# State-space loop: GpSimd multiplies two states by two C rows in one operation of 2048 columns

## What is computed

```python
def step(h, inp):
    u_t, dt_t, B_t, C_t = inp
    h = jnp.exp(dt_t[:, :, None] * A) * h + (dt_t * u_t)[:, :, None] * B_t[:, None, :]
    y = jnp.einsum('bds,bs->bd', h, C_t)
    return (h, y)
...
y = ys.transpose(1, 0, 2) + u * Dp
y = y * jax.nn.silu(z)
return y @ W_out.T
...
x = x + _L0_conv_ref(_gn(x), ...)
x = x + _L1_conv_ref(_gn(x), ...)
```

## Time and profile before

| | |
|---|---|
| median of 3 runs | 5644.61 us (5643.97 to 5648.42) |
| the profiled execution | 5637.48 us, span 5635.7 us |
| the 64 chunks | about 100 to 3440 us of the span |
| busy over the span | PE 89%, DVE 80%, POOL 80%, ACT 61% |
| TensorE's clock in the loop | granted in full (1.00), 2.4 GHz |

### The profile page before, as it was taken

How to read it: one execution, slowest core, us unless ns; L and a number is a source line. 1 busy time by engine, 2 the same in 40 slices (tenths; PEclk the granted TensorE clock), 3 DMA queues, 4 the chain that set the end, 5 groups by cost and what they waited for, 6 DMA issues and landing times. The chain is left out here.

```text
span 5635.7 us, 68281 instructions
## 1 busy us (share of the span) xinstructions
PE 5006.5 (89%) x22742; PEld 2621.1 (47%) x22742; DVE 4530.2 (80%) x6402; ACT 3450.4 (61%) x4188; POOL 4494.9 (80%) x2067
## 2 busy tenths in 40 slices
PE   6999999999999999999999997982779999899898
PEld 3444444444444444444444444530446666566565
DVE  8999999999999999999999997005767677677665
ACT  5666676676676676666566562000667777677676
POOL 6999999999999999999999995001557777677676
PEclk9999999999999999999999999795889999999999
DMA  5656666566566555565566562592789999999999
GB/s 206 211 211 212 210 211 213 209 211 215 208 211 214 208 212 214 208 212 213 209 212 214 209 212 97 216 407 50 165 156 191 195 194 192 193 193 190 189 192 184
DMA packets 1416309, 1137.13 MB, mean 202 GB/s; under 512 B 1212666, under 2 KB 1222546, under 8 KB 1408532
## 3 DMA queue, kind: packets, MB, share of 16 engines
q1 hardware_dynamic: 1411480, 1131.52, 72.2%
q10 hardware_dynamic: 4478, 1.25, 0.2%
HBM read 814.23 MB, written 21.09 MB: 148 GB/s over the span
## 5 line engine op out<-in xcount | busy, mean ns | idle before, releaser
L822 POOL TENSOR_TENSOR mamba_state<-mamba_state,mamba_c_row 128x1024 f32<-128x1024 f32 x1024 | 2404.9, 2366 | 107.3 <-DVE mamba_state L795 96.8
L693 PE MATMUL mamba_y_ps<-mamba_state,ident 128*128 128x512 f32 x4096 | 1954.4, 602 | 146.9 <-POOL mamba_state L822 145.6
L795 DVE TENSOR_TENSOR_SCAN mamba_state<-mamba_decay,mamba_b_ps 128x1024 f32<-128x1024 f32 x704 | 1609.9, 2287 | 96.3 <-DVE mamba_b_ps L781 1.9
L1957 POOL TENSOR_TENSOR l3s_el<-l3s_s_sb,l3s_eh 128x1024 f16<-128x1024 f32 x512 | 1083.3, 2135 | 473.3 <-ACT l3s_s_sb L1942 454.3
L693 PEld LDWEIGHTS mamba_y_ps<-mamba_state,ident 128*128 128x128 f32 x4096 | 744.2, 189 | 995.6 <-issue 659.2
L1965 DVE TENSOR_SCALAR_CACHE_REDUCE l3s_s_sb<-l3s_s_ps 128x512 f32<-128x512 f32 x1024 | 705.3, 690 | 453.2 <-PE l3s_s_ps L1898 447.8
L1912 PE MATMUL l3s_o_ps<-l3s_vt,l3s_et 128*128 128x257 f16 x4096 | 806.0, 275 | 132.0 <-DMA l3s_et<-l3s_el 90.9
L781 DVE TENSOR_TENSOR mamba_b_ps<-mamba_dtu,mamba_b_ps 128x1024 f32<-128x1024 f32 x704 | 849.4, 1207 | 0.6 <-PE mamba_b_ps L681 0.6
L1941 ACT ACTIVATE l3s_eh<-l3s_s_sb,l3s_shift 128x1024 f16<-128x1024 f32 x512 | 583.5, 1140 | 429.3 <-DVE l3s_shift L1976 405.7
L795 DVE TENSOR_TENSOR_SCAN mamba_state<-mamba_b_ps,mamba_b_row 128x1024 f32<-128x1024 f32 x320 | 729.1, 2278 | 103.4 <-POOL mamba_b_row L816 103.3
L771 ACT ACTIVATE mamba_decay<-mamba_dt,mamba_A 128x1016 f32<-128x1016 f32 x704 | 782.9, 1133 | 12.5 <-DVE mamba_state L795 9.4
(11 more groups left out here) (325 smaller groups left out, 5153.7 us busy)
## 6 DMA issues: line engine op xcount, KB each, us to landing
mamba_c_row<-mamba_c_rows SPq DMA_DIRECT2D x1024, 512.0 KB, 3.8
mamba_b_row<-mamba_c_rows SPq DMA_DIRECT2D x320, 512.0 KB, 4.8
l_ring_a<-in_L_conv_W SPq DMA_DIRECT2D x28, 1024.0 KB, 11.0
l2b_ring_b<-in_L_conv_W SPq DMA_DIRECT2D x26, 1024.0 KB, 11.1
l_ring_a<-in_L_conv_W SPq DMA_DIRECT2D x14, 704.0 KB, 12.7
l2b_ring_b<-in_L_conv_W SPq DMA_DIRECT2D x13, 704.0 KB, 12.7
l_ring_a<-in_L_conv_W SPq DMA_DIRECT2D x14, 640.0 KB, 12.1
l2b_ring_b<-in_L_conv_W SPq DMA_DIRECT2D x13, 640.0 KB, 12.1
```

The costliest lines, as they stand in the source:

```text
L693: last = nc.tensor.matmul(y_ps[:, half(h)], C["ident"][:, :], state[:, s % STATES, half(h)], start=False, stop=(s == S - 1))
L795: nc.vector.tensor_tensor_scan(state[:, s % STATES, :], by, add, 0.0, ALU.mult, ALU.add).then_inc(s_scan, 1)
L822: nc.gpsimd.tensor_tensor(state[:, s % STATES, :], state[:, s % STATES, :], c_row[:, s % C_ROWS, :], ALU.mult).then_inc(s_hc, 1)
L1957: nc.gpsimd.tensor_tensor(el[:, part, off:off + EXPW], s_sb[:, par, j * EXPW:(j + 1) * EXPW], eh[:, part, off:off + EXPW], ALU.subtract).t ...
```

## The change

- GpSimd's product takes two units at once: at each even unit it multiplies the states of the two units before it, which lie in neighbouring buffers, by two C rows in neighbouring buffers (2048 columns). `pool_product` does nothing for odd units. C rows are loaded as before, one transfer each, but wait and signal in pairs.
- `LAG` is 4 (was 3), `STATES` 6 (was 4), `DECAYS` 3 (was 4), `GATE_AT` 3 (was 2).
- GpSimd makes the drives of units 3, 5, 7, 9, 11 (was 2, 4, 6, 8, 10), three units ahead (was two), and their B rows are loaded five units ahead (was two), those of units 3 and 5 both at unit 0.

```diff
-LAG = 3
-PAIRS, DECAYS, STATES, C_ROWS = 2, 4, 4, 4
+LAG = 4
+PAIRS, DECAYS, STATES, C_ROWS = 2, 3, 6, 4
+DUO = 2
-GATE_AT, OUT_AT, ADD_AT = 2, 14, 15
+GATE_AT, OUT_AT, ADD_AT = 3, 14, 15
-POOL_UNITS = (2, 4, 6, 8, 10)
+POOL_UNITS = (3, 5, 7, 9, 11)
-B_ROWS, DRIVE_AHEAD, B_LOAD_AHEAD = 5, 2, 2
+B_ROWS, DRIVE_AHEAD, B_LOAD_AHEAD = 5, 3, 5
...
+        def decay_free(c, s):
+            c_of, k = divmod(by_dve(c, s) - 1 - DECAYS, len(DVE_UNITS))
+            return c_of * S + DVE_UNITS[k] + 1
...
-            wait(sp, s_hc, unit + 1 - C_ROWS)
-            sp.dma_start(c_row[:, s % C_ROWS, :], c_dram[par, s].partition_broadcast(P)).then_inc(s_crow[s % C_ROWS], 16)
+            if s % DUO == 0:
+                wait(sp, s_hc, (unit - C_ROWS) // DUO + 1)
+            sp.dma_start(c_row[:, unit % C_ROWS, :],
+                         c_dram[par, s].partition_broadcast(P)).then_inc(s_crow[unit % C_ROWS // DUO], 16)
...
-            wait(pe, s_hc, unit + 1)
+            if s % DUO == 0:
+                wait(pe, s_hc, unit // DUO + 1)
...
-                wait(act, s_scan, unit + 1 - DECAYS)
-                to = decay[:, s % DECAYS, :]
+                wait(act, s_scan, decay_free(c, s))
+                to = decay[:, decay_slot(c, s), :]
...
-            wait(pool, s_scan, unit + 1)
-            wait(pool, s_crow[s % C_ROWS], 16 * (c * S // C_ROWS + s // C_ROWS + 1))
-            nc.gpsimd.tensor_tensor(state[:, s % STATES, :], state[:, s % STATES, :], c_row[:, s % C_ROWS, :],
+            if s % DUO:
+                return
+            own, row = unit % STATES, unit % C_ROWS
+            wait(pool, s_scan, unit + DUO)
+            wait(pool, s_crow[row // DUO], 16 * DUO * (unit // C_ROWS + 1))
+            nc.gpsimd.tensor_tensor(state[:, own:own + DUO, :], state[:, own:own + DUO, :], c_row[:, row:row + DUO, :],
                                     ALU.mult).then_inc(s_hc, 1)
...
-            if s + B_LOAD_AHEAD in POOL_UNITS:
-                load_b(sp, c, par, s + B_LOAD_AHEAD)
+            for k in POOL_UNITS:
+                if s == max(0, k - B_LOAD_AHEAD):
+                    load_b(sp, c, par, k)
...
-            late = behind(c, par, s, 1)
+            late = behind(c, par, s, DUO)
```

More of the change, by code:

```diff
@@ L577, in mamba_layers @@
         s_bdrive = sem(f"{tag}_pool_drive_ready")
-        s_crow = [sem(f"{tag}_c_row_loaded_{i}") for i in range(C_ROWS)]
+        s_crow = [sem(f"{tag}_c_rows_loaded_{i}") for i in range(C_ROWS // DUO)]
         s_hc = sem(f"{tag}_hc_ready")
@@ L690, in pe_sum @@
                     nc.tensor.matmul(y_ps[:, half(h)], weights(c)["diag_Dp"][:, :], u[:, par, half(h)], start=True, stop=False)
-            wait(pe, s_hc, unit + 1)
+            if s % DUO == 0:
+                wait(pe, s_hc, unit // DUO + 1)
             for h in range(2):
-                last = nc.tensor.matmul(y_ps[:, half(h)], C["ident"][:, :], state[:, s % STATES, half(h)], start=False,
+                last = nc.tensor.matmul(y_ps[:, half(h)], C["ident"][:, :], state[:, unit % STATES, half(h)], start=False,
                                         stop=(s == S - 1))
@@ L793, in dve_scan @@
                 wait(dve, s_drive, by_dve(c, s))
-                by, add = decay[:, s % DECAYS, :], b_ps[s % PAIRS][:, :]
-            nc.vector.tensor_tensor_scan(state[:, s % STATES, :], by, add, 0.0, ALU.mult, ALU.add).then_inc(s_scan, 1)
+                by, add = decay[:, decay_slot(c, s), :], b_ps[s % PAIRS][:, :]
+            nc.vector.tensor_tensor_scan(state[:, unit % STATES, :], by, add, 0.0, ALU.mult, ALU.add).then_inc(s_scan, 1)
         def dve_gate(dve, c, par):
@@ L951, in _ @@
                 run(pool, pool_unit)
-                pool_product(pool, LAST, LAST % 2, S - 1)
+                pool_product(pool, LAST, LAST % 2, S - DUO)
 GRID = 4
```

6 lines of the change are left out of this document (4 added, 2 removed).

## The result

The changed kernel takes 5675.48 us (median of 5 runs, 5671.87 to 5679.78), beside 5643.97 us for the kernel before (5 runs, 5640.04 to 5648.42): a ratio of 1.0056, 95% interval 1.0042 to 1.0071. It is slower by 31.5 us. The forecast was 5667 us, slower by 22, within a range of 5612 to 5700.

A forecast was written before the change was run, and what follows sets the result against it. It took TensorE, VectorE and GpSimd as nearly full, bound by a VectorE-GpSimd loop of 52.82 us a chunk. Loop +12, norm chunks +6 and the end +4 make +22 us: 5667 us, range 5612 to 5700.

The forecast's parts named there:

- the term of the loop: Chunk period from gate to gate over 63 periods: 53.01 us against 52.82, +12 us in all.
- The pair's price: GpSimd's 2048-column product, start to start: 4.47 us taken, upper bound 4.63, lower bound 3.55.
- The bound of 3.55: Lower bound in us for GpSimd's pair product, from the only 2048-column row (3595 ns); not taken.
- rival 1: GpSimd's pair is cheap: at the 3.55 bound a chunk takes 51.7 us, the kernel 5584 us; chance 0.15.
- The old loop: GpSimd's products delay its drives for VectorE's scans; opening it would leave VectorE's 51.07 us floor, 110 us less.
- The new chain: Gate to gate through GpSimd's pairs up to (8,9), then TensorE's queue to sum 15: 28.4 + 14.0 + 10.6 = 53.0 us.
- VectorE's side waits: VectorE waits for late B rows 8, 12, 13, 15; with these it alone would reach the gate at 52.3 us.
- rival 3: Nothing decides: pair at 4.42 us or slack in TensorE's chain, within 11 us of before, some 5650 us; chance 0.24.
- Norm chunks: TensorE's norm products behind the out product come onto the path, in 14 and 7 chunks: +6 us.
- The end: After the last scan a whole pair and two sums follow instead of one product and one sum: +4 us.
- Rival 2: TensorE is not late at the gate; B rows 13 and 15 set 52.3 us a chunk, 5622 us; chance 0.08.
- Rival 4: Four loads together are late, GpSimd starts pair (0,1) late: 1 us a chunk gives 5730 us; chance 0.08.

The follow-up runs named there:

- run 2: The changed kernel with one product a unit instead of pairs, everything else of the change kept: 5581.99 us, ratio 0.9893 to the kernel before.
- Run 1: The changed kernel with two idle TensorE matmuls put ahead of the sum of unit 6: 5648.42 us, ratio 1.0011 to the kernel before.
- run 11: The changed kernel with single products, TensorE also waiting before sum 6 for VectorE's drive of unit 10: 5743.89 us, ratio 1.0180 to before.
- run 9: Changed kernel, single products; bc product ahead of sum 1, dt product and sum 3 behind B row 8, GpSimd's first product after VectorE's norm operations: 5569.44 us.
- run 8: The changed kernel, pairs kept, with sums five units behind instead of four and the gate at 4: 5751.83 us, ratio 1.0190 to before.
- run 4: The changed kernel with the z product of the preparation moved ahead of sum 6 in TensorE's queue: 5736.01 us, ratio 1.0169 to before.
- run 5: The changed kernel with the z product ahead of sum 6 and the out product ahead of sum 8: 5683.16 us, ratio 1.0071 to before.
- run 10: The changed kernel with single products, TensorE's sum of an even unit still waiting for the next unit's product: 5582.01 us, ratio 0.9894 to before.

## Why the prediction was right, and where it was not

It forecast the sign, the mechanism and the place, and the time within 8.5 us. That the time came so near is in part luck: one large term was missing, and the term of the loop was too large.

- **The pair's price.** p = 4.47 forecast; from start to start the rows give 4.48 to 4.50, 4540 ns by the group. The bound of 3.55, and with it rival 1, is out. The figure of the Trainium skill (GPSIMD Engine Reference, section on performance versus the Vector engine), 4497 ns for this size, is 43 ns below the mean here.
- **The old loop opens.** Right: VectorE no longer waits for GpSimd's drives, and run 2 shows that the new places without the pair are worth 1 us a chunk.
- **The new chain, step by step** (clean chunk, gate at 2792.06). Pair (2,3) after 3.50 (3.48 forecast). TensorE sees pair (8,9) at 28.49 (28.4). B row 1 starts 13.71 later (14.0). Sum 15 ends 10.52 after that (10.54). The gate comes at 52.76 (53.0). VectorE's side waits were 0.43 at drive 8, 0.32 at 12 and 0.17 at 13 (0.6 and 0.1 to 0.3 each forecast). GpSimd idles 2.11 before pair (14,15) (2 forecast). B row 15 was in time. The chain is 0.25 shorter than the sum of pitches, the largest piece of it in the turn (0.36 us from start to start, 0.50 forecast), so the loop's +12 us is -3 (63 x -0.05). That is the term that was mis-sized: a difference of 15 us, the distance between rival 3 and the forecast.
- **Norm chunks.** +6 forecast. Run 1, whose loop is clean, has 63 periods from first scan to first scan with a mean of 52.95 over 52.77, 11.5 us; before has 52.87 over 52.82, 3.3. So +8.
- **The end.** +4 forecast, +3.9 measured: from the start of the last scan to the last gate are 10.66 us instead of 6.78. The intervals from gate to gate hide it (the last is 50.13 in run 1 and 50.29 before), because the gate of the chunk before has moved by one unit. VectorE's last scan and last gate, before and then changed:

```profile
3435.02 2.29 DVE L795 TENSOR_TENSOR_SCAN mamba_state<-mamba_decay,mamba_b_ps 128x1024 f32<-128x1024 f32 x1
3441.80 1.22 DVE L801 TENSOR_TENSOR mamba_yz<-mamba_sz,mamba_y_ps 128x1024 f32<-128x1024 f32 x1 [4.50 <-PE mamba_y_ps L693]
```

```profile
3472.44 2.29 DVE L808 TENSOR_TENSOR_SCAN mamba_state<-mamba_decay,mamba_b_ps 128x1024 f32<-128x1024 f32 x1
3483.09 1.22 DVE L814 TENSOR_TENSOR mamba_yz<-mamba_sz,mamba_y_ps 128x1024 f32<-128x1024 f32 x1 [8.37 <-PE mamba_y_ps L706]
```

- **The missing step: TensorE's clock.** The prediction took all of TensorE's rows at full clock. It named the wait for the pair only as the start of the deciding chain and never said how long TensorE stands still there. The holes around these sums were 0.8 to 1.1 us before (the two below, from a plain chunk); now the one before sum 6 is 1.3 to 2.0. Run 1 removes the clock's loss by filling this hole (28.5 us back from gate to gate), run 11 makes the loss without a pair. This is the largest part of the 41.4 us.

```profile
2884.17 1.98 PE L693 MATMUL mamba_y_ps<-mamba_state,ident 128*128 128x512 f32 x4 [0.91 <-POOL mamba_state L822]
...
2891.11 1.99 PE L693 MATMUL mamba_y_ps<-mamba_state,ident 128*128 128x512 f32 x4 [0.92 <-POOL mamba_state L822]
```

- **The prologue.** +3.3 us before the first scan, not forecast. It goes with the start of GpSimd's first product (dt u of chunk 0), at 51.51 us instead of 48.78. In the profiles of the changed kernel and of all runs but 9, whose programs do the same work up to there, that start lies anywhere between 48.50 and 51.75, and the first scan follows it by 6.4 to 6.9 us (6.0 before). So most of the 3.3 can be scatter from execution to execution; it is not shown to be the change's. The rest of the first gate's +7.5 is the gate's later place (3.5) and the longer first chunk.
- **The sum of what was measured,** by first scans: plain chunks -3.2, norm chunks +8.3, the end +3.9 less 0.5 in the scans of the last chunk, the half clock +28.0 over the 63 periods and +1.5 in the last chunk (changed kernel less run 1), the prologue +3.3, behind the last gate +0.1: 41.4. The forecast's +22 came near the medians' +31.5 with a different make-up: without the clock the kernel would have ended at "nothing decides" (rival 3), as run 1 does with 1.0011.
- **Rival 2**, that TensorE is not late at the gate, was nearer than its 0.08 said: the wait before the gate is 0.34 in clean chunks, not 0.7, and in half-clock chunks (1.99 at drive 12) it is VectorE, held by one B row, that closes the period. **Rival 4** is out: GpSimd waited 1.0 us for C rows and 1.3 for B rows in all.

What stays open: which of the holes of 1 to 2.6 us lower the clock in a given chunk. The hole before sum 6 of the changed kernel did in 33 chunks (1.55 to 2.00 us) and did not in 29 (1.27 to 1.99); 1.98 did in 39 chunks of run 8, 2.64 in 54 of run 4, 2.58 in 58 of run 11, and two of 1.16 and 0.76 close together in 32 of run 5. A single one of 1.37 (run 1), 1.29 (run 10) or 1.68 (run 9, in nearly every chunk) did in none. The runs do not give a rule.
